# Keys and values of a top-k attention projected between the rounds of the query selection

## The reference, cut to what matters

```python
h = _layernorm(x) * (1 + ca) + sa                 # ca, sa: rows of silu(c) @ wmod
Q, K, V = proj(Wq, bq), proj(Wk, bk), proj(Wv, bv)  # y = h @ W.T + b, 32 (batch, head) pairs of 2048 x 16
query_norms = jnp.linalg.norm(Q, axis=2)
_, top_idx = jax.lax.top_k(query_norms, 409)
Q_sel = jnp.take_along_axis(Q, top_idx[:, :, None], axis=1)
scores = jnp.einsum('bud,bld->bul', Q_sel, K) * scale
out_sel = jnp.einsum('bul,bld->bud', jax.nn.softmax(scores, axis=-1), V)
out_full = zeros.at[arange(BH)[:, None], top_idx].set(out_sel)
x = x + ga * (out @ Wo.T + bo)
x = x + gb * experts(_layernorm(x) * (1 + cb) + sb)   # top 2 of 8
```

## Time and profile before

| | us |
|---|---|
| median of 3 runs (range) | 1120.99 (1120.28 to 1122.05) |
| profiled execution | 1120.14 |
| its span | 1118.3 |
| PE busy | 907.3 (81%) |
| DVE busy | 879.3 (79%) |
| ACT busy | 595.5 (53%) |
| POOL busy | 581.5 (52%) |

### The profile page before, as it was taken

One profiled execution on the slowest core, in us unless ns is written; L12 is line 12 of the kernel. 1 busy time (PEld: TensorE's weight loads), 2 busy tenths in 40 slices (PEclk: granted clock), 3 DMA queues, 4 the chain that ended last, 5 costly groups with the idle time before them and its releaser, 6 DMA issues. The chain is left out here.

```text
span 1118.3 us, 26572 instructions
## 1 busy us (share of the span) xinstructions
PE 907.3 (81%) x7725; PEld 569.2 (51%) x7726; DVE 879.3 (79%) x2070; ACT 595.5 (53%) x1351; POOL 581.5 (52%) x595
## 2 busy tenths in 40 slices
PE   7999300269999999999757722999999999999995
PEld 4444100212333333333346521877778888888884
DVE  4795688898999999997368876677787777777774
ACT  2565185308888888888534413544544444444441
POOL 2354374253777777763699821254454454545443
PEclk9999755557999999999889955999999999999998
DMA  7334673110111111120279812889943232323232
GB/s 244 105 128 155 221 232 119 28 42 20 25 39 24 38 24 40 30 73 23 75 208 263 253 33 59 240 225 219 225 90 48 48 47 47 52 42 53 41 48 29
DMA packets 125021, 110.55 MB, mean 99 GB/s; under 512 B 17489, under 2 KB 114449, under 8 KB 124945
## 3 DMA queue, kind: packets, MB, share of 16 engines
q1 hardware_dynamic: 102816, 86.76, 25.8%
q0 software_dynamic: 20480, 21.53, 11.8%
q10 hardware_dynamic: 1648, 1.31, 0.4%
HBM read 50.98 MB, written 35.50 MB: 77 GB/s over the span
## 5 line engine op out<-in xcount | busy, mean ns | idle before, releaser
L993 DVE TENSOR_REDUCE attend_mxh<-attend_p_a 128x1 f32<-128x512 f32 x416 | 258.6, 678 | 4.2 <-PE attend_p_a L1176 2.7
L1106 ACT ACTIVATE w<-attend_p_b 128x409 f32<-128x409 f32 x512 | 227.4, 515 | 44.1 <-PE attend_p_b L1190 43.4
L1914 ACT ACTIVATE expert_hr<-expert_p,b1t 128x256 f32<-128x256 f32 (+1 forms) x376 | 134.4, 423 | 194.0 <-PE expert_p L1852 177.5
L1807 POOL DMA_INDIRECT out_x<-expert_ys,expert_drop x72 | 121.6, 1689 | 191.9 <-DVE expert_ys L1949 133.4
L1874 PE MATMUL expert_p<-w,expert_hhi 128*128 x800 | 136.6, 273 | 0.5 <-DVE expert_ys L1949 0.3
L1852 PE MATMUL expert_p<-expert_xhi,w 128*128 128x256 f16 x800 | 136.4, 273 | 0.0
L1176 PE MATMUL attend_p_a<-w,attend_qa 64*128 64x512 f16 x384 | 123.2, 407 | 11.1 <-DVE attend_mxh L993 9.8
L1190 PE MATMUL attend_p_b<-attend_qb,w 64*128 64x409 f16 x512 | 130.4, 344 | 1.8 <-ACT w L1106 1.4
L918 POOL DMA_INDIRECT attend_qsel<-q_d,idx x96 | 91.5, 953 | 53.7 <-DVE attend_mxh L993 44.0
L1216 PE MATMUL attend_p_o<-w,attend_vh 128*32 128x409 f32 x1024 | 115.3, 523 | 0.7
L933 POOL DMA_INDIRECT attn_d<-outs,idx x90 | 89.1, 990 | 49.8 <-DVE attend_mxh L993 31.4
(11 more groups left out here) (350 smaller groups left out, 1770.7 us busy)
## 6 DMA issues: line engine op xcount, KB each, us to landing
expert_wu<-w SPq DMA_DIRECT2D x88, 256.0 KB
w<-in_L_ffn_w SPq DMA_DIRECT2D x20, 512.0 KB, 4.3
q_d<-project_q SPq DMA_DIRECT2D x32, 256.0 KB, 2.0
x<-in_L_attn_x SPq DMA_DIRECT2D x8, 512.0 KB, 10.1
attn_d<-zero SPq DMA_DIRECT2D x8, 512.0 KB
w<-k_d SPq DMA_DIRECT2D x32, 128.0 KB
route_ain<-attn_d SPq DMA_DIRECT2D x32, 128.0 KB
route_xin<-in_L_attn_x SPq DMA_DIRECT2D x32, 128.0 KB, 2.6
```

What stands on the lines that cost most here:

```text
L993: dve.tensor_reduce(mxh[q % 2][:, h, c, k:k + 1], p_a[chunk_use(q, a, h) % CB][:, :], AX, ALU.max).then_inc(a_done, 1)
L1106: act.activation(prob[:, 2 * (j % (TPB // 2)) + h, :], p_b[tile_use(p, j, h) % TB][:, 0:TOP], ACT.Exp, scale=SCALE / UNIT ** 2).then_inc(p ...
L1807: pool.indirect_dma_start(out=out, out_offset=bass.IndirectOffsetOnAxis(ap=drop[u][:, s:s + 1], axis=0), in_=ys[u][:, s, :], in_offset=Non ...
L1914: last = act.activation(hr[g % 2][:, f, rows], p_1[g][:, f, rows], ACT.Relu, bias=cst["b1t"][:, bass.ds(e[s] * FB + 2 * g + f, 1)], scale= ...
```

## The change

1. `project_block` projects queries alone (256 columns a tile). The turned rows `ht` of all 32 tiles stay in SBUF, in the place that the upper half of the expert weights w1 takes later. ACT normalises (Identity with scale and shift per row) instead of DVE. The four modulation matmuls come at tiles 2, 4, 6 and 8, and the fix of their signs moves to the end of `attend_block` on DVE. After the last tile PE computes two of the 16 pairs of value tiles.
2. `select_block`: on PE, after the count matmul of each round, come one unit of keys (256 output rows in two halves, 512 rows of x each: `keys(u)`, 16 units) and one tile of values. ACT makes the first part of the keys (`high_key`), copies the values, and splits the 16 weights in between; POOL makes the second part; SP saves each unit between the weight loads. DVE's one-hot tables wait for all keys saved and all values computed.
3. A row of `q3_d` has 32 float16 (HELD = 2: first part, second part). In `turned` one piece of a head is 32 wide, the other 16 wide with an added matmul that clears its 32 rows. The key rows in SBUF are laid out to match.
4. V's bias is added in `spread_v` on POOL. The 13 small constant loads move from `select_block` to `attend_block`, ahead of its weight loads.

```diff
-HELD = 4
+HELD = 2
+V_FIRST = 2
@@ project_block, DVE
-                    dve.tensor_scalar(h[t % R][:, :], x[:, t, :], mv[j % 2][:, i, 0:1], rstd[j % 2][:, i:i + 1], ALU.subtract, ALU.mult).then_inc(h_done, 1)
-                    dve.tensor_tensor(cst["v"][:, t % TPB, b, :], p_qv[t % 2][:, D:2 * D], biasb[:, b, D:2 * D], ALU.add).then_inc(v_done, 1)
-                unrolled([norm, None, None, None, evacuate, squares, modulation])
+                unrolled([ahead, None, None, evacuate, squares])
@@ project_block, ACT
+                    act.activation(h[t % R][:, :], x[:, t, :], ACT.Identity, bias=shift[j % 2][:, i:i + 1], scale=rstd[j % 2][:, i:i + 1]).then_inc(h_done, 1)
-                unrolled([None, None, copy_ht, None, first, None, last_of_block(first_k)])
+                unrolled([norm, copy_ht, None, None, first])
+                for m in range(V_FIRST):
+                    values(m)
@@ project_block, PE
-                        last = pe.matmul(p_qv[t % 2][:, :], ht[t // BLK % 2][:, k, t % BLK, :], wtb[:, t // TPB, k, 0:2 * D], start=(k == 0), stop=(k == KD - 1))
+                        last = pe.matmul(p_q[t % 2][:, 0:D], ht[:, k, t, :], wtq[:, t // TPB, k, :], start=(k == 0), stop=(k == KD - 1))
-                unrolled([None, turn_h, None, project, last_of_block(project_k)])
+                unrolled([turn_h, None, project])
@@ select_block, SP
+                for i in range(WR):
+                    load(i)
+                loads = itertools.count(WR)
+                for u in range(UNITS_K):
+                    save(u)
+                    if u % 4 != 3:
+                        load(next(loads))
@@ select_block, POOL
+                for u in range(UNITS_K):
+                    low_key(u)
+                    if u % 4 != 3:
+                        low_weight(next(weights))
@@ select_block, ACT
+                def high_key(u):
+                    bias = bkb[:, u % 2, u // 2 * KT // L:u // 2 * KT // L + 1]
+                    act.wait_ge(k_ps, u + 1)
+                    wait(act, klo_done, u - 1)
+                    act.activation(yk[u % 2], p_k[u % 2][:, :], ACT.Identity, bias=bias).then_inc(yk_done, 1)
+                    wait(act, k_saved[u % 2], 16 * PARTS * (u // 2))
+                    act.activation(k3[u % 2][:, 0, :], p_k[u % 2][:, :], ACT.Identity, bias=bias).then_inc(khi_done, 1)
+                for u in range(UNITS_K):
+                    high_key(u)
+                    if u % 4 != 3:
+                        high_weight(next(weights))
+                    if u % 2:
+                        values(V_FIRST + u // 2)
@@ select_block, PE
+                def keys(u):
+                    j, oc = divmod(u, 2)
+                    b = j * KT // L
+                    wait(pe, yk_done, u - 1)
+                    wait(pe, khi_done, u - 1)
...
+                keys(0)
+                values(next(tiles))
                 for i in range(PAIRS):
                     pe.wait_ge(cnt_done, i + 1)
                     pe.matmul(p_c[:, 0:3], same[:, :], cnt[:, 0:3], start=True, stop=True).then_inc(cnt_ps, 1)
+                    keys(i + 1)
+                    values(next(tiles))
@@ select_block, DVE, ahead of the one-hot tables
+                dve.wait_ge(v_ps, NT // 2 - V_FIRST)
+                for i in range(2):
+                    dve.wait_ge(k_saved[i], 16 * PARTS * UNITS_K // 2)
@@ attend_block
-                    pool.tensor_copy(vh[p % 2][:, :, :, 0:HD], vn[:, :, 2 * p:2 * p + 2, :]).then_inc(vh_done, 1)
+                    pool.tensor_tensor(vh[p % 2][:, :, :, 0:HD], vn[:, :, 2 * p:2 * p + 2, :], bv[:, 2 * p:2 * p + 2, :].unsqueeze(1).broadcast_to([P, TPB, 2, HD]), ALU.add).then_inc(vh_done, 1)
+                                if r:
+                                    pe.matmul(into[32 * w:32 * w + 32, cols], mpart[0:k, h, c, :] if low else blank[:, :], cst["identb"][0:k, 0:cols.stop - cols.start],
+                                              start=True, stop=False, tile_position=(0, 32 * w))
```

More of the change, by code:

```diff
@@ L508, in _, with modulation @@
+                for m in range(V_FIRST):
+                    values(m)
             @block.tensor
             def _(pe):
+                def modulation(i):
+                    b, c = divmod(i, 2)
+                    if i == 0:
+                        pe.wait_ge(cst["rows_here"], 16)
+                    wait(pe, mod_done, i - 1)
+                    for k in range(KD):
+                        last = pe.matmul(p_mod[i % 2][:, :], cst["silub"][:, k * B + b, :], cst["wmod"][:, k, (c + 1) * 512:(c + 2) * 512], start=(k == 0), stop=(k == KD - 1))
+                    last.then_inc(mod_ps, 1)
@@ L515, in turn_h @@
                     last.then_inc(h_ps, 1)
+                    if t in MOD_AT:
+                        modulation(MOD_AT.index(t))
                 def project(t):
@@ L570, in select_block @@
         p_c = ps("p_c", [P, 512], F32)
-        p_t = [ps(f"p_t{i}", [P, P], F32) for i in range(SEG)]
+        p_tt = ps("p_tt", [P, SEG, P], F32)
+        p_t = [p_tt[:, i, :] for i in range(SEG)]
         ramp = sb("ramp", [P, TPB * GH, SLOT_L], F16)
@@ new lines, in values @@
+                def values(m):
+                    b, i = divmod(2 * m, TPB)
+                    act.wait_ge(v_ps, m - V_FIRST + 1)
+                    act.activation(cst["v"][:, i:i + 2, b, :], p_v[m % 2][:, :, :], ACT.Copy).then_inc(v_done, 1)
+                weights = itertools.count(WFIRST)
+                for u in range(UNITS_K):
[4 more added lines that the diff above has]
+                        values(V_FIRST + u // 2)
@@ L660, in _ @@
+                pairs = itertools.count(V_FIRST + UNITS_K // 2)
+                for i in weights:
+                    if i >= WLAST:
+                        break
+                    for m in itertools.islice(pairs, 2):
+                        if m < NT // 2:
+                            values(m)
+                    high_weight(i)
                 act.wait_ge(lanes_ready, 1)
@@ new lines, in build_program @@
+                    sizes = dict(wmod=KD * 6 * D, silub=KD * B * P, wtq=B * KD * D, biasq=B * D)
+                    ends = list(itertools.accumulate(sizes.values()))
+                    part = {name: low[:, end - size:end] for (name, size), end in zip(sizes.items(), ends)}
+                    cst.update(wmod=part["wmod"].rearrange("p (k n) -> p k n", k=KD), silub=part["silub"].rearrange("p (k n) -> p k n", n=P),
+                               wtq=part["wtq"].rearrange("p (b k n) -> p b k n", b=B, k=KD), biasq=part["biasq"].rearrange("p (b n) -> p b n", b=B))
```

329 lines of the change are left out of this document (157 added, 172 removed).

## The result

The changed kernel takes 1125.2 us (median of 12 runs, 1121.0 to 1129.4) beside 1121.0 for the kernel before on the same chip: ratio 1.0036, 95% interval 1.0021 to 1.0050. It is slightly slower; the forecast was 1098, range 1088 to 1116. The profiled execution took 1124.8 us, its span is 1123.0.

A forecast was written before the change was run, and what follows sets the result against it. PE was taken to bound the projection, DVE the selection's rounds and the attention, with ACT setting the selection's pace after the change. 1120.1 - 41.5 (projection) + 17.5 (selection) + 1 (attention) = 1097, stated as 1098 us; range 1088 to 1116.

The forecast's parts named there:

- Projection: Projection block: without the key and value matmuls it ends sooner, selection starting 41.5 us earlier (37 to 45).
- Handovers: Projection: three nearly equal engines lose something at every handover, so 1.5 us a tile (1.35 to 1.8).
- its terms up to the barrier: Projection: start 22.0, tiles 48, modulation 6.9, last tile 2, values 3.4 and 1.2, barrier 1.8; block end at 84.
- Attention: Attention block: 1 us longer in all (0 to 3), with V's bias on POOL costing nothing.
- The added matmuls in the turns: Attention, `turned`: 8 more small matmuls in 16 calls, up to 7 us of PE, taken as 1 (0 to 3).
- The sign fixes: End of attention: nine DVE instructions, 6 us in all, hidden in DVE's 8.56 us wait for the last result.
- Selection: Selection block: ends at 104 us against 86.4, 17.5 us longer; ends 99 and 116.
- the stall: Selection: the first weight's load, behind the clears, delays the fourth count to 26 us from 14.2; about 12 us lost.
- The rounds behind it: Selection after the fourth count: ACT's list sets the pace, 3.1 to 3.7 us a round, last count at 60 us.
- PE stays at the lower clock: Rival, selection: clock stays at 1.2 GHz, every round waits for PE, selection 49.5 us longer, total 1129; chance 0.06.
- The stretched selection: Rival, selection: late saves make rounds 4 us instead of 3.3, 12 us more, total 1110; chance 0.20.

The follow-up runs named there:

- the wait: POOL's spread of V waits until DVE has moved that pair's tails' maxima: 1096.7 us on the changed kernel, 1112.2 us on the kernel before.
- the splits moved away: Changed kernel, output clears behind the last weight load, V's spread behind DVE's moved tails, plus POOL's last four weight splits behind the lane comparisons: 1084.0 us.
- clears last and reductions: Changed kernel, output clears issued behind the last weight's load and DVE's three tail copies made reductions: 1083.7 us on a usual chip, 1169.1 on the slower.

## Why the prediction was wrong

- **Projection, right.** -42.6 against -41.5. Handovers cost less than I took (1.37 us a tile, not 1.5), the start with its modulation rows more: 20 to 30 has PE at 5.78 of 10 us and a clock of 0.66. So it is right in part by errors that cancel. The working also has a slip: its terms up to the barrier, with ACT's 1.2 us, add to 85.3 and not 84; the block ended at 83.0.
- **Attention, the step that failed**: "V's bias makes 16 copies on POOL two-input instructions of 512 columns, at most 1.18 us each; POOL's gathers and scatters are paced by DVE's maxima, so nothing". I asked who waits for POOL and found nobody. The time of one instruction was mis-sized a little (1.27 us for "at most 1.18"), the effect on the others was put at nothing. I didn't ask what runs on DVE at the same time: copies of 25 x 2 elements that already took 314, 466 and 335 ns, where alone they take 156. The traces split the +21.2 us: 12 periods are longer by 0.9 us, 11 us, as POOL's longer instruction holds DVE up longer (pause 2.14 for 1.27), and one of these by another 1.0, as the kernel before had no collision in it; six of them are longer by another 1.5 us, 9 us, as the clock falls behind PE's wait. Without the bias most of it is gone, 1125.2 - 1106.9 = 18.3 us; with the wait, which also takes away most of the collision that the kernel before had, the time falls by 28.5.
- **The added matmuls in the turns, nearly right**: I took 1 us (0 to 3). With the wait in both, the attention is 329.4 in the changed kernel and 325.8 in the kernel before: 3.6 us for all the other changes in it, a little over the range. No run has these matmuls alone. The sign fixes stayed hidden, as forecast: from the last `minus_maximum` to route's first matmul it is 25.9 us, before 26.1.
- **Selection, the term was mis-sized**: 26.1 for 17.5, a selection of 112.5 us, near the long end of 116. The mechanism and the stall were as worked out, to 0.1 us. The rounds behind it gave 5 us more than forecast (3.53 us each, for 3.1); ACT's waits for saves, 7.9 us in all, are in them, and what makes the saves late stays open. Behind the last count another 3 us came on the way to the positions: 1.7 in the product and 0.4 in the cast L765, both held up by POOL's splits (with the splits moved away they are gone), and 0.8 in L753 (1.53 us for 0.69), which lies beside POOL's last part of the keys and which no run took away. Of the 3.8 us in the column comparisons about 1.3 counts: DVE ends its lanes 2.5 us behind ACT, where the working has 1.2. It is the same step left out as in the attention: I had POOL's and DVE's lists, and priced each alone.
- **The rivals.** "PE stays at the lower clock" had something like the right mechanism in the wrong block: from the fourth count to the last the clock stood at 1.00, and it fell in the attention, where I expected no change of it. The stretched selection came true in good part (+8.6, where it has +12). With +8.6 the forecast would have been 1107, and the version without the bias takes 1106.9; that they agree to a tenth is luck, as the attention of that version is still 1.6 us over the forecast and its route and experts 2.4 us longer than before. No rival had the attention.

## What to carry to other kernels

Before a DVE and a POOL instruction are made longer, or given a second input in SBUF, look for what the other of the two does at that time: on this kernel the second input of a 1.3 us instruction, on an engine with nobody waiting for it, cost 18 to 28 us. A tiny instruction whose mean is two or three times what one of its shape takes alone (466 ns for 156 here) is the sign of it. An ordering wait, or another form of the small instruction, removed it here at no cost. When an engine that PE waits for gets later, look at PE's granted clock, in windows, and not only at the wait's length.

## What the runs showed of the hardware

- DVE's copy between SBUF tiles of 25 x 2 elements took 0.16 us alone and up to 1.98 beside POOL's gather and two-input instruction, with which it ended; the means of the maxima from PSUM (677 to 679 ns) were the same in all versions. A reduction of the same 25 x 2 elements took 0.14 to 0.15 us beside gathers and, in two cases, beside the start of the two-input instruction.
- A float32 two-input instruction of 512 columns on POOL takes 1275 ns, a copy 616 to 619.
- DVE's two-input instructions were held up by POOL's as well: a product of 512 columns took 2437 ns beside POOL's splits and 692 without them.
- On the usual chips the granted clock of PE, once it had risen near the start of the attention (264 us in the kernel before), stayed at 2.4 GHz through the periods of the versions in which PE waited up to 0.26 us for DVE's maxima. In those in which it waited 0.8 to 1.1 us once a period it fell to 1.2 GHz for a part of six to ten periods, each of which was 1.5 us longer. Why in these periods and not in the others stays open.
- One chip of those used ran the kernel before in 1195 us and the version with clears last and reductions in 1169, with a clock of 0.83 to 0.91 in the attention's windows although DVE's maxima pause only 0.42 us there. So a late DVE is not the only thing that goes with a lower clock. Why was not looked into.
